# A fused attention and state-space kernel: first sample's bf16 remainders on VectorE, its first row of maxima in two halves, late inputs loaded at other places, and a reordered hand-over to the scan

## The reference

```python
# layer 0: attention whose weights are modulated by a style vector
x = x * s1[:, None, :]
x = (x - mean(x)) * rsqrt(var(x) + 1e-5)
q, k = heads((x @ Wq.T) * q_dc), heads((x @ Wk.T) * k_dc)      # 16 heads of 16 channels
v_flat = (x @ Wv.T) * v_dc * s2
out = softmax(q @ k.T * 0.25) @ heads(v_flat)
x1 = x_in + (out @ Ww.T) * w_dc + (v_flat @ Wu.T) * u_dc       # dc = rsqrt(square(W) @ square(s) + eps)
# layer 1: causal convolution, layernorm, a clipped recurrence over the 256 steps
xr, gate = split(x1 @ W_in.T)                                  # 512 channels each
xn = layernorm(silu(conv4(xr + t_emb)))
Bm, Cm, dt = split(xn @ W_xproj.T)                             # 16 states each
Bd = Bm * minimum(norm(xn), 1)                                 # per token
h = clip(h * Ad[t] + Bd[t] outer xn[t], -10, 10)               # t = 0..255
y = Cm[t] . h + D * xn[t]
return x1 + (y * silu(gate)) @ W_out.T
```

## Time and profile before

| what | value |
|---|---|
| median of 3 runs | 542.61 us |
| the profiled execution | 539.56 us, span 537.8 us |
| TensorE busy | 475.2 us (88%) |
| VectorE busy | 432.0 us (80%) |
| ScalarE, GpSimd busy | 256.8 us (48%), 177.5 us (33%) |
| chain that ended last | PE 51%, DVE 31%, DMA 6%, ACT 6%, issue 3% |
| granted TensorE clock, mean | 0.978 of full |

### The profile page before, as it was taken

The page is one execution under the profiler, slowest core; times in us unless marked ns, Lnnn a source line. Parts: engine busy times, 40 slices in busy tenths (PEclk is TensorE's granted clock), DMA queues, the critical chain, the costliest instruction groups (busy, mean ns, idle before and its releaser), DMA issues.

```text
span 537.8 us, 8609 instructions
## 1 busy us (share of the span) xinstructions
PE 475.2 (88%) x3062; PEld 286.3 (53%) x3082; DVE 432.0 (80%) x754; ACT 256.8 (48%) x512; POOL 177.5 (33%) x197
## 2 busy tenths in 40 slices
PE   6977699899999899888999888789999999999996
PEld 6744466768677566567887553233333333333333
DVE  6966257686766777749997977989999999999994
ACT  3442578757677546777777667343311111111111
POOL 5744303303023000000730002698783334333332
PEclk8879799999999999999999998999999999999999
DMA  8158864563545710110066377675546333333310
GB/s 313 39 177 212 318 175 90 153 173 92 138 109 135 177 40 2 41 40 1 2 247 195 110 247 175 223 239 195 165 138 157 117 117 112 107 104 105 105 37 22
DMA packets 45607, 71.81 MB, mean 134 GB/s; under 512 B 19098, under 2 KB 34074, under 8 KB 42893
## 3 DMA queue, kind: packets, MB, share of 16 engines
q1 hardware_dynamic: 37924, 65.64, 41.4%
q0 software_dynamic: 528, 3.55, 1.7%
q10 hardware_dynamic: 7112, 2.08, 1.6%
HBM read 41.88 MB, written 23.02 MB: 121 GB/s over the span
## 4 chain that ended last, share of the span: by engine, by line
PE 51%; DVE 31%; DMA 6%; ACT 6%; issue 3%; POOL 1%; ACTq 1%; SPq 0%; DVEq 0%
DVE win L1834 11%; PE bank L1023 6%; PE bank L1467 6%; PE bank L1079 5%; PE bank L1427 5%; PE bank L1438 5%; PE bank L1049 5%; PE bank L1064 5%; DVE z L1834 4%; PE bank L1128 3%; PE bank L1106 3%; DVE acc L1621 3%; DVE mx L1643 2%; PE bank L1097 2%; DVE zlast L1834 2%
## 5 line engine op out<-in xcount | busy, mean ns | idle before, releaser
L1643 DVE TENSOR_REDUCE mx<-bank 128x2 f32<-128x512 f32 x128 | 81.7, 686 | 61.0 <-PE bank L1049 60.9
L1427 PE MATMUL bank<-xst,bst 128*128 128x512 bf16 x238 | 76.3, 387 | 21.6 <-DVE win L1834 10.5
L737 ACT ACTIVATE ex<-bank 128x512 f32<-128x512 f32 x128 | 70.9, 599 | 40.8 <-PE bank L1064 40.8
L1834 DVE CUSTOM_DVE_ANT_0 win<-win,bank,hi 128x512 f32<-128x512 f32 x96 | 71.8, 748 | 3.4
L1427 PEld LDWEIGHTS bank<-xst,bst 128*128 128x128 bf16 x256 | 24.6, 97 | 70.7 <-DVE win L1834 31.9
L501 POOL TENSOR_TENSOR qk<-qk,part 128x512 f32<-128x512 f32 x16 | 21.9, 1372 | 108.9 <-ACT part L662 108.9
L1023 PE MATMUL bank<-xnT,w 128*128 128x256 f32 x192 | 51.1, 421 | 3.7 <-ACT xnT L647 1.8
L1064 PE MATMUL bank<-qst,kst 128*128 128x256 bf16 x256 | 46.8, 277 | 7.6 <-DMA qst<-mT 5.9
L1049 PE MATMUL bank<-kst,qst 127*128 127x256 bf16 x256 | 47.2, 277 | 6.3 <-DVE mx L1643 6.0
L605 POOL TENSOR_TENSOR yg<-yT,gateT 128x128 f32<-128x128 f32 x60 | 29.2, 519 | 57.3 <-ACT yT L956 57.3
L1023 PEld LDWEIGHTS bank<-xnT,w 128*128 128x128 f32 x192 | 39.5, 213 | 10.9 <-ACT xnT L647 2.5
(11 more groups left out here) (209 smaller groups left out, 917.7 us busy)
## 6 DMA issues: line engine op xcount, KB each, us to landing
qk_d<-part SPq DMA_DIRECT2D x60, 96.0 KB, 2.4
xs_d<-xpart SPq DMA_DIRECT2D x15, 384.0 KB, 4.7
xst<-xs_d SPq DMA_DIRECT2D x15, 384.0 KB
xn_d<-xc SPq DMA_DIRECT2D x16, 256.0 KB, 3.9
xtk<-xn_d SPq DMA_DIRECT2D x64, 64.0 KB
xst<-xs_d SPq DMA_DIRECT2D x15, 256.0 KB
bd_d<-zeros POOLq DMA_DIRECT2D x1, 3468.0 KB, 13.0
qst<-qk_d SPq DMA_DIRECT2D x7, 384.0 KB, 4.0
```

Source lines behind the costliest of these rows:

```text
L737: nc.scalar.activation(ex[:, n // 4, n % 4, :], bank[6 + n % 2][:, :], ACT.Exp, scale=SCALE)\
L1427: mm(bank[t % 4][:, :], bst[:, slot, t % RS, :], xst[slot][:, t % RS, :], start=True, stop=True)\
L1643: v.tensor_reduce(mx[:, :, STACKED[n]:STACKED[n] + 1], bank[4 + n % 2][:, :].rearrange("p (t k) -> p t k", t=HALVES), AX.X, ALU.max)\
L1834: v._custom_dve(bass.dve_ops.TENSOR_ADD_SAT, out=zst[t % ZR], in0=zst[(t - 1) % ZR], in1=bank[t % 4][:, :], s0=hi[:, t:t + 1], s1=0.0).the ...
```

## The change

- **SP:** `xres` is loaded right behind the small weights, ahead of the first sample's stacks; `win`, `lnr`, `tA` and `wo` go behind the third stack and its arrival.
- **First sample:** its four subtractions move from GpSimd to VectorE, between the steps of a rearranged prologue: the style products of the 12 later tiles are cut into 2, 4 and 6, and their statistics come behind the demodulation factors. GpSimd sets `vp` and `ones` only behind the first sample's parts.
- **Maxima of sample 0:** after 8 of the 16 maxima TensorE turns them (`turn_first_half`), ScalarE copies and sends half a row (`take_first_half`); `scores(0, 0, 2)` then run before the last two maximum scores. The other half follows from `take_maxima(0)`, and is waited for at score 8.
- **Split of the 8 tiles:** the first part is cast by VectorE (`first_part`), the third by ScalarE (`third_part`); the norms are taken earlier in ScalarE's program, the table for the gates is loaded behind the last third part.
- **Hand-over to the scan:** the first load of B is issued half on ScalarE's queue and half on SP's; SP's stores and loads there are reordered.

```diff
-def load_b(eng, i, name, lo=0, hi=RS):
+def load_b(eng, i, name, lo=0, hi=RS, groups=(0, 1)):
-    for at, row, count in ((0, 0, 27), (33, 27, 24)):
+    for at, row, count in [((0, 0, 27), (33, 27, 24))[j] for j in groups]:
         rows = bd_d[row * BP:(row + count) * BP].rearrange("(r t c) -> r t c", r=count, c=P)
...
+    sp.dma_start(xres[:, :, :], xT).then_inc(s["ld_x"], 16)
     def load_stack(b, lo, hi, done):
...
     stack(1)
-    sp.dma_start(xres[:, :, :], xT).then_inc(s["ld_x"], 16)
+    stack(2)
+    sp.wait_ge(s["ld_q2"], 48)
+    sp.wait_ge(s["ld_k2"], 48)
     for dst, src in ((win[:, :, :], winT), (lnr[:, :, :], ln_row.partition_broadcast(P)),
...
         sp.dma_start(dst, src).then_inc(s["ld_l2"], 16)
-    stack(2)
     for b in range(1, B):
...
     store_parts(B - 2)
-    store_xn(B - 1)
+    store_parts(B - 1, 0, FIRST, "xs_first")
     sp.wait_ge(s["bsplit"], 1)
     store_b(sp, 0, range(3), 0, RS, "bd_first")
-    store_parts(B - 1, 0, FIRST, "xs_first")
-    store_parts(B - 1, FIRST, RS, "xs_second")
     parts_stored(B - 1)
...
     load_x(0, "ld_xf", 0, FIRST)
-    sp.wait_ge(s["xs_second"], 16)
-    load_x(0, "ld_x0", FIRST)
     sp.wait_ge(s["bd_first"], 16 * 7)
+    load_b(sp, 0, "ld_bf", 0, FIRST, (1,))
+    store_parts(B - 1, FIRST, RS, "xs_second")
+    store_xn(B - 1)
     load_b(sp, 0, "ld_b0", FIRST)
+    sp.wait_ge(s["xs_second"], 16)
+    load_x(0, "ld_x0", FIRST)
     store_parts(B - 1, RS, P)
...
     nc.gpsimd.memset(kst[:, :, :, :], -1.0).then_inc(s["stacks_clear"], 1)
-    pool.wait_ge(s["dc_done"], 1)
+    pool.wait_ge(s["part_ready"], 2)
     own.mark(nc.gpsimd.memset(vp[:, :, :, :, :], 1.0))
...
-    for b in range(B):
+    for b in range(1, B):
         if b == 2:
...
+    def take_first_half():
+        act.wait_ge(s["mt_half"], 1)
+        nc.scalar.activation(mT[0:NH // 2, :], bank[3][0:NH // 2, 0:S], ACT.Copy).then_inc(s["mT_half"], 1)
+        act.wait_ge(s["mT_half"], 1)
+        act.dma_start(qstacks[0][M_ROW:P, 0:NH // 2], mT[0:NH // 2, :]).then_inc(s["m_half"], 16)
     def take_maxima(b):
...
         act.wait_ge(s["mt_done"], b + 1)
+        if b == 0:
+            act.wait_ge(s["m_half"], 16)
         nc.scalar.activation(mT[:, :], bank[3][0:NH, 0:S], ACT.Copy).then_inc(s["mT_ready"], 1)
         act.wait_ge(s["mT_ready"], b + 1)
-        act.dma_start(qstacks[b % NBUF][M_ROW:P], mT[:, :]).then_inc(s["m_row"], 16)
+        lo = NH // 2 if b == 0 else 0
+        act.dma_start(qstacks[b % NBUF][M_ROW:P, lo:], mT[lo:, :]).then_inc(s["m_row"], 16)
...
             take_xn(b + 2, 2)
+        if b == 0:
+            exponentials(0, 0, 2)
         take_maxima(b)
...
             take_qk(b + 2, 0, 2)
-            if b == 0:
-                exponentials(0, 0, 2)
             take_qk(b + 2, 1, 3)
...
     act.wait_ge(s["rt_in"], 4)
-    nc.scalar.activation(rt[:, 2 * HALVES:], var_e[:, 2 * HALVES:], ACT.Sqrt).then_inc(s["rt_out"], 1)
-    act.wait_ge(s["rt_in"], 5)
     nc.scalar.activation(dct[:, 2:, :, :], dcv[:, 2:, :, :], ACT.Sqrt).then_inc(s["rt_out"], 1)
...
     second_cast(1, 1)
+    act.wait_ge(s["rt_in"], 5)
+    nc.scalar.activation(rt[:, 2 * HALVES:], var_e[:, 2 * HALVES:], ACT.Sqrt).then_inc(s["rt_out"], 1)
     take_vt(1, 3)
     nc.scalar.activation(minus[:, :], ident[:, :], ACT.Copy, scale=-1.0).then_inc(s["minus_ready"], 1)
+    take_first_half()
     for b in range(B):
...
         b, t = FINISHED[j]
+        if j < B:
+            act.wait_ge(s["xn_ready"], j + 1)
         if j >= 1:
...
+    def third_part(j):
+        act.wait_ge(s["left_ready"], j + 1)
+        nc.scalar.activation(xpart[:, j % XRING, 2, :], bank[6 + j % 2][:, :], ACT.Copy)\
+            .then_inc(s["parts_ready"], 1)
     def second_part(j):
...
-    leave_parts(0)
     square(0)
     take_gate(3)
-    leave_parts(1)
     second_part(0)
     square(1)
-    leave_parts(2)
     second_part(1)
+    third_part(0)
     square(2)
-    leave_parts(3)
+    third_part(1)
     square(3)
+    second_part(2)
+    second_part(3)
+    third_part(2)
+    third_part(3)
     nc.scalar.activation(warm[:, :], ones[:, 0:1], ACT.Sqrt)
...
         .then_inc(s["ipct_ready"], 1)
-    second_part(2)
     act.wait_ge(s["yb_done"], 1)
     nc.scalar.activation(ybias[:, :], bank[1][:, 0:R], ACT.Copy).then_inc(s["ybias_ready"], 1)
-    for j in range(4, B):
-        leave_parts(j)
-        second_part(j - 1)
-        if j in (5, 6):
-            split_d(j - 4)
+    square(4)
+    second_part(4)
+    for j in range(5, B):
         square(j)
-    act.wait_ge(s["sq_done"], B)
-    nc.scalar.activation(nrm[:, 0, :], ss[:, 0, :], ACT.Sqrt).then_inc(s["nrm_ready"], 1)
+        if j == B - 1:
+            act.wait_ge(s["sq_done"], B)
+            nc.scalar.activation(nrm[:, 0, :], ss[:, 0, :], ACT.Sqrt).then_inc(s["nrm_ready"], 1)
+        third_part(j - 1)
+        second_part(j)
+        if j < B - 1:
+            split_d(j - 4)
+    third_part(B - 1)
     nc.scalar.activation(warm[:, :], ones[:, 0:1], ACT.Silu)
-    second_part(B - 1)
-    take_gate(4)
     act.wait_ge(s["zfill"], 16)
...
     store_b(act, 0, range(3, 6), 0, RS, "bd_first")
+    take_gate(4)
     act.wait_ge(s["bd_first"], 16 * 7)
-    load_b(act, 0, "ld_bf", 0, FIRST)
+    load_b(act, 0, "ld_bf", 0, FIRST, (0,))
     take_gate(5)
...
-        if lo == 0:
+        if b == 0 and lo == 0:
+            pe.wait_ge(s["m_half"], 16)
+        if lo == (NH // 2 if b == 0 else 0):
             pe.wait_ge(s["m_row"], b * 16 + 16)
...
         pe.wait_ge(s["maxes"], b * NH + NH)
+        if b == 0:
+            pe.wait_ge(s["mT_half"], 1)
         for t in range(HALVES):
...
+    def turn_first_half():
+        pe.wait_ge(s["vt_in"], 2)
+        pe.wait_ge(s["maxes"], NH // 2)
+        for t in range(HALVES):
+            ins = nc.tensor.transpose(bank[3][0:NH // 2, t * P:(t + 1) * P], mx[:, t, 0:NH // 2], ident[:, :])
+        ins.then_inc(s["mt_half"], 1)
     def project_att(b, bk):
...
         channels_of(1, 3, "k_done")
-        scores(b, 0, 2)
+        if b >= 1:
+            scores(b, 0, 2)
         max_scores(b + 1, 0, 2)
...
     channels_of(2, 3, "vt_done")
-    pe.wait_ge(s["rt_in"], 5)
+    pe.wait_ge(s["rt_in"], 4)
     max_scores(0, 0, 8)
...
     pe.wait_ge(s["wgain"], 1)
+    max_scores(0, 8, 10)
+    turn_first_half()
     weight_sums()
-    max_scores(0, 8, 12)
+    max_scores(0, 10, 12)
     pe.wait_ge(s["k_in"], 2)
...
     channels_of(0, 2, "q_done")
+    scores(0, 0, 2)
     max_scores(0, 14, NH)
...
     second_left(1)
-    project_gate(4)
+    first_left(2)
+    first_left(3)
+    second_left(2)
+    project_gate(4, 0, 2)
+    second_left(3)
+    project_gate(4, 2, 4)
     pe.wait_ge(s["ipc_ready"], 1)
...
     ins.then_inc(s["eb_back"], 1)
-    first_left(2)
...
     ins.then_inc(s["yb_done"], 1)
-    second_left(2)
     left_of_d(0)
-    first_left(3)
-    project_gate(5, 0, 1)
-    second_left(3)
     first_left(4)
...
     first_left(5)
-    project_gate(5, 1, 2)
+    project_gate(5, 0, 1)
     second_left(5)
...
     first_left(6)
+    project_gate(5, 1, 2)
     second_left(6)
...
-    def modulated_statistics(lo, hi):
+    def modulate(lo, hi):
...
             own.mark(v.tensor_tensor(xt[:, n, :], xt[:, n, :], s1b[:, n // HALVES, :], ALU.mult))
+    def modulated_statistics(lo, hi):
+        modulate(lo, hi)
         statistics(xt, lo, hi)
...
     normalise(1, False)
+    dve.wait_ge(s["cast0"], 1)
+    v.tensor_tensor(qk[:, 0, :], qk[:, 0, :], part[:, 0, 0, :], ALU.subtract).then_inc(s["rem_qk"], 1)
     dve.wait_ge(s["ld_rest"], 32)
-    modulated_statistics(2 * HALVES, NT)
+    modulate(2 * HALVES, 3 * HALVES)
+    dve.wait_ge(s["cast0"], 2)
+    v.tensor_tensor(qk[:, 1, :], qk[:, 1, :], part[:, 1, 2, :], ALU.subtract).then_inc(s["rem_qk"], 1)
+    for w in range(2):
+        dve.wait_ge(s["cast1"], w + 1)
+        v.tensor_tensor(part[:, w, 2 - 2 * w, :], qk[:, w, :], part[:, w, 1, :], ALU.subtract)\
+            .then_inc(s["part_ready"], 1)
     dve.wait_ge(s["dcsum"], 2)
     demodulate(2, 5, 5)
-    dve.wait_ge(s["rt_in"], 5)
-    dve.wait_ge(s["rt_out"], 5)
+    modulate(3 * HALVES, 5 * HALVES)
+    dve.wait_ge(s["rt_in"], 4)
+    dve.wait_ge(s["rt_out"], 4)
     rsqrt(dc[:, 2:, :, :], dct[:, 2:, :, :], dcv[:, 2:, :, :], dct[:, 2:, :, :])
...
     v.memset(tick[:, :], 0.0).then_inc(s["dc_done"], 1)
-    roots(2 * HALVES, NT, 4)
+    modulate(5 * HALVES, NT)
+    statistics(xt, 2 * HALVES, NT)
+    roots(2 * HALVES, NT, 5)
     dve.wait_ge(s["const_pool"], 1)
...
+    def first_part(j):
+        b, t = FINISHED[j]
+        dve.wait_ge(s["xn_ready"], j + 1)
+        if j >= XRING:
+            dve.wait_ge(s[f"xs_out{j % XRING}"], 16 * (j // XRING))
+        v.tensor_copy(xpart[:, j % XRING, 0, :], xc[:, b * HALVES + t, :]).then_inc(s["part0"], 1)
     def finish(tiles):
...
     scale(0, first)
-    finish((1,))
+    later = centre(1)
+    first_part(0)
+    scale(1, later)
```

(21 more changed lines are left out.)

8 lines of the change are left out of this document (4 added, 4 removed).

## The result

| | runs | median us | range us | profiled execution, its span |
|---|---|---|---|---|
| before | 20 | 541.75 | 539.91 to 543.48 | 539.56, 537.8 |
| after | 20 | 544.63 | 541.07 to 548.00 | 542.99, 541.2 |

After against before: **1.0052, with a 95% interval of 1.0035 to 1.0069**. The change makes the kernel slower by 0.5%, about 2.8 us; I had forecast 5.5 us less. The range of its runs is twice as wide as that of before, which turned out to be a clue. The profiled execution of before is faster than all 20 of its runs in the table, that of after lies 1.6 us under its median; differences between the two profiles are therefore not differences between the medians.

The account below looks back on a forecast made before the run. The prediction saw a chain of waits as the bound, with TensorE busy 88% and VectorE 80%. Early part -5.95 us plus hand-over +0.4 gave -5.5 us, from a median of 542.61 to 537.1 us, range 534.4 to 540.2.

Parts of the forecast that it names:

- step 1: First sample's parts: stores and stacks come 4.3 us earlier, but VectorE's first maximum starts 0.5 us later.
- step 3: Sample 0's row no longer holds up TensorE: -8.0 us to the v projection's end, then +0.4 and +0.3 behind it.
- rival B: VectorE and GpSimd collide, or half clock paces the first maxima: first maximum 2.3 us later, 538.9 us; chance 0.20.
- Step 2: Maxima of sample 0: reductions take as long as before, the added half turn and two scores cost +0.85 us.
- Rival E: Slower: the late loads meet the row of sample 1 and TensorE's clock drops again, 544.5 us; chance 0.08.
- Step 4: Hand-over to the scan: casts moved off VectorE, B's stores later, third slot's wait longer; +0.4 us, bounds -1.5 and +2.5.

Follow-up runs that it names:

- b_prologue: Kernel before with only sample 0's four subtractions on VectorE, the statistics behind them and ScalarE's last root behind the second casts; 1.0078, 545.50 us.
- a_hold: Changed kernel, old loads' place, ScalarE's root first, 40 filling matmuls, gaps filled, sample 1's stack loads held until the half row landed; 0.9949, 538.44 us.
- a_order: Changed kernel with loads at their old place and the last six samples' statistics again ahead of the second demodulation's root; 1.0033, 542.82 us.
- b_half: Kernel before with only sample 0's row of maxima sent in two halves; 0.9931, 537.29 us.
- H: The part of the change that sends sample 0's row of maxima in halves; alone on the kernel before 0.9931, 537.29 us.
- T: The part of the change that reorders the hand-over to the scan; alone on the kernel before 0.9981, 540.26 us.
- P: The prologue part of the change: subtractions on VectorE, statistics behind them; alone on the kernel before 1.0078, 545.50 us.
- L: The part of the change that moves the place of SP's loads; alone on the kernel before 1.0020, 542.06 us.
- a_spread: Changed kernel with win, lnr with tA, and wo loaded one after another behind the stacks of samples 4, 5 and 6; 1.0024, 543.86 us.
- b_tail: Kernel before with only the hand-over to the scan reordered; 0.9981, 540.26 us.
- a_fixed_warm: Changed kernel, ScalarE's root first, late loads behind sample 4's au and sr moves, 40 filling matmuls where TensorE awaits the first maximum; 0.9969, 539.21 us.
- half_tail: Kernel before with the half row and the reordered hand-over, without the other two parts; 0.9890, 537.06 us.
- a_fixed_dense: a_fixed_warm with one more matmul in each gap of sample 0's maximum scores 2 to 7; 0.9970, 540.07 us.

## Why the prediction was wrong

Two steps failed where it counts: step 1 put the whole prologue at +0.5 us, and by runs it costs 4.8; step 3 put the late loads at nothing, and they cost 4 to 5.

**Step 1** had the order right and one term wrong that its profile shows. I put the wait for the roots at 0.75 us, "behind ScalarE's four store issues". The trace of before could have told me that the root also stands behind ScalarE's copy of sample 1's channels, which waits for TensorE. It is 2.16 us in the profile after and 3.67 in b_prologue. The +0.5 was +1.4, or +4.4 in the other clock, at the first maximum. In the end time the prologue costs 4.8 us (0.9979 against 0.9890), of which a_hold, with the three known causes removed, shows 1.6 us back (0.9949 against 0.9979, and these two intervals overlap). The rest stays open. Of rival B a trace remains: `var_e` took 0.61 us where the same operation takes 0.17 in a_order, and ended at 35.11, just behind GpSimd's subtractions (35.08).

**Step 2** failed in the changed kernel's profile. "Sixteen reductions take as long as before" holds at TensorE's upper level alone; b_half, which has it, shows the +0.66 (50.75 against 50.09) for my +0.85. In the changed kernel the level was the lower one and the term +5.0 (17.67 against 12.65). I had read the clock only where TensorE waited for the row. Of these 5 us only a part can stand between the medians, since most runs of the kernel before probably have the lower level too (57 of 138 at 0.968 or less, 12 at the 0.978 of the profile I read); how large a part, no run shows.

**Step 3**, the row's wait, went as forecast in its place: turn to the end of the v projection 5.0 us (5.2 forecast, 13.2 before). Two of its clauses were wrong. The stacks' slack was to shrink, for +0.3: b_half shows +3.0 in sample 1, since the row of sample 1 now meets the loads of sample 2's stack. And "the au and sr moves queue behind them and have a whole sample of slack" left out who is behind the moves: the copy into `pvc` and, on SP's queue, the whole stack of sample 3. That clause is worth 0.7 to 1.0%, 4 to 5 us. Rival E had the loads as the danger, but named the row of sample 1; that row waited 0.63 us. It is the queue's later work that paid.

**Step 4** had the wrong sign and a small size: +0.4 forecast, -1.0 us measured (0.9981). The cast was well sized: 0.42 us at the median for my 0.45. My term that B's stores leave 1.3 us later on ScalarE does not show: the chain of waits there goes through ScalarE's third part of the last tile (321.07) and SP's stores and loads.

**Summing up:** from 541.75 us, H and T give -6.0 (0.9890), P on top of them +4.8 (0.9979) and L on top of all +4.0 (1.0052), which makes the +2.8 us measured. The forecast had -6.75 for H and the row (-8.0 + 0.85 + 0.4), +0.5 for P, +0.3 for L and +0.4 for T.

Of the row I had said that by the Trainium skill (DMA: Bandwidth & Descriptors, "Queues, rings and completion order") a row on a queue of its own would hardly wait. The measured rows stand against that: 5.8, 6.7 and 7.4 us behind loads on SP's queue, 1.8 us otherwise. The same section has a second rule that I should have taken: the increment of a semaphore lands only after every earlier write of that DMA engine, across its queues. All of these rows agree with it; none can tell it from other reasons for which a row would wait for loads issued just ahead.

## What to carry to other kernels

Before a transfer is moved, list what stands behind it on the same queue and who waits for that, and what small transfers of any queue are sent just behind it (4 us in a_spread): the largest costs of this change were not the moved bytes but the next sample's stack and a row of 8 to 16 numbers per token. Work that an engine does while it waits for another is cover; moving the work behind the wait turns an unsteady neighbour (here a clock) into one's own time, and a wider spread of runs can be the sign of it. Before a profile is taken as the baseline, compare its mean clock and its time with those of the other runs: here the one I read was faster than all 20. Try the parts of a change alone: here the half row held nearly all of the gain, and two other parts gave it away.

## What was not expected of the hardware

- The granted clock of TensorE in the same stretch of the same program differs between executions: before and b_tail, whose programs differ only from layer 1 on, have 1.00 and 0.50 from 43 to 46 us (and 1.00 and 0.57 from 22 to 26). With the old prologue it is 1.00 in four and 0.50 in three profiles from 43 to 46 us, and the turn comes 3.1 to 4.4 us later for it (53.20 and 54.25 against 50.09, 55.02 against 50.62). It fell in a_fixed_warm while each pair took 0.39 of 0.60 us, and stayed up in half_tail with the same pairs; one added matmul of 0.117 us in each gap kept it up in three profiles of four; in the fourth TensorE had idled 2.50 us just ahead. The Trainium skill (TensorE: Matmul & The Clock Gate, "What's actually happening") says that the level follows the engine's recent activity; these rows agree, and add that it is not only whole idle stretches that bring it down (a_fixed_warm had idled 0.64 us).
- A row of maxima of 4 or 8 KB lands in 1.8 us (the median of before) or in up to 7.4 us (a_fixed_dense), by what was issued on another queue in the 3 us ahead of it.
- VectorE's product of 12 columns (`rt<-rs`, 40.11) took 1.12 us instead of 0.17 and ended at 41.23 us, with GpSimd's subtractions (38.93 + 2.27 = 41.20). The Trainium skill (SBUF — State Buffer, "SBUF: two separate sides") has it so for an operation with two SBUF inputs beside a GpSimd operation that reads SBUF: an exclusive lock to the end of the instruction. The row agrees.
